# Context statistics through DRAM, and two normal forms of the context made from its transposed copy

## The chip, the cores and the metric

The kernel runs on one core of one Trainium2 chip. The metric is the device time of one execution in microseconds, given as the median of several runs. Batches of the work go through the core one behind the other in an overlapped pipeline, so the steady time of one batch counts 64 times.

## What is computed

There are 64 sequences (`B`) of 128 rows (`S`) and 256 features (`D`), an input `x` and a context of the same shape, and all arithmetic is fp32. Four cross-attention layers stand in a row. Cut to what matters here:

```python
# layer 0: two 16-head attentions (x on x, then x1 on context), three layer norms, fc1/fc2
# layer 1:
h  = rmsnorm(x, ln1_w);  kv = rmsnorm(context, ln1_w)
k, v = kv @ Wk, kv @ Wv                      # 4 key/value heads of 64, rope on q and k
x  = x + attention(h @ Wq, k, v) @ Wo;  x = x + (silu(n @ Wgate) * (n @ Wup)) @ Wdown   # n = rmsnorm(x)
# layer 2:
q  = layer_norm(x);      c  = layer_norm(context, gkv, betakv)
K, V = c @ Wk + bk, c @ Wv + bv
x  = x + attention(q @ Wq + bq, K, V) @ Wo + bo
# layer 3: attention on the plain context with a mask factor and a clip, then a layer norm
```

So the context is wanted in four forms: times a 0/1 row mask (layer 0, second attention), RMS-normed (layer 1), layer-normed (layer 2) and plain (layer 3). The gains and offsets of the norms are folded into weights and biases at the start.

## The kernel before, in words

**Batches.** One batch is one sequence. Its activations stay in SBUF in one of `G` = 4 slots (`g = b % 4`). The attentions are numbered `a` = 0 to 4. Each step of a batch is an event: `queries`, `keys`, `scores`, `soft` (mask, maximum and exponentials, in four units), `turn` (transposes of a unit's probabilities, four units), `values`, `attended` (transposes back and the division), `zT` and `o` (output projection), `tr` (transposes of the inputs of the next attention), and for the dense parts `q2`, `kv2`, `o2`, `x2T`, `h`, `z`, `nT`, `gate`, `up`, `down`. Below, "turn 2.3" is the event `turn` of attention 2, unit 3.

**Order.** The order on each engine is written out by hand. `LIFE` (line 76) gives every event a number for each engine that it uses. `order(engine)` (line 205) adds `PERIOD * b` for batch `b`, sorts all events of all batches, and each engine's program walks through its own sorted list. The numbers only sort; they are no times of the chip. At one time four batches are in work. TensorE's program is `tensor_program`, and the other four queues wait on semaphores for it and for each other.

**PSUM.** Everything but scores goes through `gen_ps`, `N_GEN` = 4 banks in turn, in the order of TensorE's list. A bank's next use waits until its reader has released it (`begin`, `bank_read`); the names in `BANK_LATE` ask for the bank before the other waits of their step.

**The context before.** `ctx_norms` on VectorE makes mean and variance of each context row (lines 1061 to 1066), on GpSimd it makes two factors (`crstd`, line 788) and the RMS-normed context `ctx_rms` (line 809), row by row in the layout rows x features. `tr 2` on TensorE transposes two halves of `zn` (the query side) and two halves of `ctx_rms` (the helper `transposes`, line 459, says line 459 for every transpose), ScalarE copies all four out (`copy_out`, line 699, 512 wide), and `q2` and `kv2` (helper `product`, line 467) multiply them with weights. When `tr 2` has read `ctx_rms`, `ctx_ln` on GpSimd writes the layer-normed context into the same buffer (line 814), and `tr 3` transposes `zn` and that. Attention 4 takes the plain context from `ctxT`, which is loaded already transposed. `x_in`, the loaded `x`, shares the buffer of `ctx_rms`, and `add_residual` (line 796) is its last reader.

**GpSimd's other work.** Each norm takes its reciprocal root from GpSimd (line 788), in the events `stats`, `z`, `mean_square`, `down` and `o 4`; `q2` and `kv2` there finish the rotation, `prob_norm` (line 849) divides the probabilities of attention 2, and `down` and `o 3` prepare the next residuals (lines 856, 860). VectorE's norms in between are `norm` and `norm_x3` (lines 945 and 948), `rms_norm` (line 1096) and `norm_x4` (line 1127).

**Loads.** SyncE waits for a finished output (line 1180), stores it, and then issues six loads for the batch that takes the slot (lines 1155 to 1162).

```python
                elif name == "tr" and a == 2:
                    pe.wait_ge(sem("n3"), b + 1)
                    pe.wait_ge(sem("ctx_rms"), b + 1)
                    transposes("tr2", b, halves(zn[:, g, :]) + halves(ctx_rms[:, g, :]))
```

## Time and profile before

| | |
|---|---|
| median of 3 runs | 4097.45 us (4096.05 to 4101.04) |
| the profiled execution's own time | 4097.15 us |
| its span, first to last instruction | 4095.3 us |
| granted TensorE clock, mean | 0.989 |
| TensorE busy (PE) | 3961.5 us, 97% |
| weight loads (PEld), beside PE | 3439.0 us, 84% |
| VectorE busy | 2890.5 us, 71% |
| ScalarE busy | 2659.4 us, 65% |
| GpSimd busy | 1231.2 us, 30% |
| data moved by DMA | 69.61 MB, mean 17 GB/s |

The busy shares are means over the whole span. PE and PEld are two halves of TensorE: the matmuls proper and the loads of their stationary operand, which run ahead beside them. Matmuls overlap each other, so a group's mean duration is longer than the step from one to the next; the step is read from the start times of a timeline. A fp32 matmul leaves two records, a transpose one.

### The profile page before, as it was taken

To read this page: it belongs to the slowest core of one execution; us is meant where nothing else is said; L and a number is where in the kernel's file an instruction comes from. 1 tells how busy PE (TensorE), PEld (TensorE's weight loads), DVE (VectorE), ACT (ScalarE), POOL (GpSimd) and SP (SyncE) were. 2 spreads that over 40 slices of the span, in tenths; PEclk is the share of its full clock that TensorE was granted. 3 is DMA by queue.
4 is the path that set the end of the run, shared out by engine and by line. 5 is a ranking of instruction groups with operands and counts; after the bars stand their busy time and mean duration, and the time that the engine had idled before them with its cause. 6 is when DMAs were issued, how large, how long until landed. Compare 5 with 4: busy or idle time off the path is not lost.

```text
span 4095.3 us, 115148 instructions
## 1 busy us (share of the span) xinstructions
PE 3961.5 (97%) x44448; PEld 3439.0 (84%) x44448; DVE 2890.5 (71%) x10721; ACT 2659.4 (65%) x8449; POOL 1231.2 (30%) x2247
## 2 busy tenths in 40 slices
...
DMA packets 66495, 69.61 MB, mean 17 GB/s; under 512 B 7456, under 2 KB 64800, under 8 KB 65056
## 3 DMA queue, kind: packets, MB, share of 16 engines
...
q14 instruction: 188, 1.54, 0.1%
...
## 4 chain that ended last, share of the span: by engine, by line
PE 55%; DVE 32%; issue 7%; POOL 3%; ACT 3%; DMA 1%; SPq 0%; DVEq 0%; POOLq 0%; ACTq 0%
PE gen_ps L467 34%; PE gen_ps L459 10%; DVE masked L971 4%; DVE negmax L977 4%; PE scores_ps L549 3%; PE gen_ps L601 3%; DVE st L937 2%; DVE zn L932 2%; DVE masked L964 2%; PE gen_ps L589 2%; PE scores_ps L556 2%; PE scores_ps L563 2%; POOL rstd L788 1%; POOL res L796 1%; DVE rdenm L929 1%
## 5 line engine op out<-in xcount | busy, mean ns | idle before, releaser
L467 PE MATMUL gen_ps<-actT,w_sb 128*128 128x128 f32 x10752 | 1390.1, 279 | 28.9 <-DVE wide L1110 13.5
L467 PEld LDWEIGHTS gen_ps<-actT,w_sb 128*128 128x128 f32 x10752 | 1285.8, 192 | 107.2 <-issue 51.5
L699 ACT ACTIVATE probT<-gen_ps 128x512 f32<-128x512 f32 x1024 | 585.5, 642 | 293.8 <-PE gen_ps L459 293.8
L788 POOL TENSOR_TENSOR rstd<-ve,consts 128x1 f32<-128x1 f32 x448 | 282.6, 631 | 1521.2 <-DVE ve L939 772.1
L733 ACT ACTIVATE prob<-scores_ps,negmax 128x128 f32<-128x128 f32 x2048 | 561.6, 432 | 189.3 <-DVE negmax L977 189.3
L459 PE MATMUL gen_ps<-consts,prob 128*128 128x128 f32 x4096 | 594.4, 278 | 16.1 <-ACT prob L733 6.4
L459 PEld LDWEIGHTS gen_ps<-consts,prob 128*128 128x128 f32 x4096 | 469.8, 142 | 129.2 <-ACT prob L733 58.2
L699 ACT ACTIVATE actT<-gen_ps 128x256 f32<-128x256 f32 (+1 forms) x512 | 235.7, 460 | 383.8 <-PE gen_ps L459 377.3
L467 PE MATMUL gen_ps<-w_sb,actT 128*128 128x256 f32 x1792 | 465.4, 383 | 3.8 <-ACT actT L699 2.8
L849 POOL TENSOR_SCALAR prob<-prob,rden 128x128 f32<-128x128 f32 x1024 | 358.8, 372 | 358.6 <-DVE rden L1050 358.6
L467 PE MATMUL gen_ps<-w_sb,wide 128*128 128x256 f32 x2056 | 465.7, 379 | 0.8 <-DVE wide L1117 0.4
L467 PEld LDWEIGHTS gen_ps<-w_sb,wide 128*128 128x128 f32 x2056 | 385.9, 190 | 51.4 <-issue 1.0
L730 ACT ACTIVATE prob<-masked,negmax 128x128 f32<-128x128 f32 x1024 | 396.0, 394 | 0.0
L977 DVE TENSOR_REDUCE negmax<-scores_ps 128x4 f32<-128x512 f32 x512 | 329.4, 685 | 90.6 <-ACT prob L733 60.0
L467 PEld LDWEIGHTS gen_ps<-w_sb,actT 128*128 128x128 f32 x1792 | 308.4, 192 | 28.9 <-ACT actT L699 4.1
L727 ACT ACTIVATE prob<-masked,negmax 128x128 f32<-128x128 f32 x1024 | 311.9, 394 | 7.3 <-DVE negmax L964 7.3
L589 PE MATMUL gen_ps<-probT,v 128*32 128x128 f32 x8192 | 279.3, 277 | 7.5 <-ACT probT L722 5.1
L699 ACT ACTIVATE oT<-gen_ps 128x512 f32<-128x512 f32 x256 | 154.1, 602 | 189.3 <-PE gen_ps L589 189.3
L1104 DVE TENSOR_TENSOR xs<-gen_ps,xs 128x256 f32<-128x256 f32 x64 | 27.2, 425 | 335.9 <-PE gen_ps L467 335.9
L589 PEld LDWEIGHTS gen_ps<-probT,v 128*32 128x32 f32 x8192 | 209.7, 110 | 45.4 <-issue 20.7
L964 DVE CUSTOM_DVE_ANT_0 masked<-scores_ps,mask 128x128 f32<-128x128 f32 x1024 | 228.9, 286 | 5.4 <-PE scores_ps L549 4.0
L964 DVE CUSTOM_DVE_ANT_0 masked<-scores_ps,consts 128x128 f32<-128x128 f32 x1024 | 228.8, 280 | 2.6 <-PE scores_ps L563 2.6
...
## 6 DMA issues: line engine op xcount, KB each, us to landing
actT<-xT_dram SPq DMA_DIRECT2D x64, 128.0 KB, 2.2
ctx_rms<-x_dram SPq DMA_DIRECT2D x64, 128.0 KB, 2.2
ctx<-ctx_dram SPq DMA_DIRECT2D x64, 128.0 KB, 2.3
ctxT<-ctxT_dram SPq DMA_DIRECT2D x64, 128.0 KB, 2.3
mask<-mask_dram SPq DMA_DIRECT2D x128, 64.0 KB, 2.1
out_dram<-res SPq DMA_DIRECT2D x64, 128.0 KB, 1.7
w_sb<-weights_dram SPq DMA_DIRECT2D x2, 2048.0 KB, 18.6
...
```

The source lines that it names most:

```text
L459: last = nc.tensor.transpose(ps[:, k * P:(k + 1) * P], src, ident)
L467: last = nc.tensor.matmul(ps, lhsT(c), rhs(c), start=(c == 0), stop=(c == chunks - 1))
L589: last = nc.tensor.matmul(ps[32 * k:32 * k + 32, u * S:(u + 1) * S], v16[:, b % G, HU * u + k, :], probT[:, u, k, :], start=True, stop=True)
L699: release(nc.scalar.activation(dst, take(act, name, b)[:, 0:width], ACT.Copy), name, b)
L727: ins = nc.scalar.activation(prob[:, N % 4, k, :], masked[:, N % 3, k, :], ACT.Exp, bias=negmax[:, N % 4, k:k + 1], scale=-1.0)
L730: ins = nc.scalar.activation(prob[:, N % 4, k, :], masked[:, N % 3, k, :], ACT.Exp, scale=-1.0, bias=negmax[:, N % 4, k:k + 1], accum_out= ...
L733: ins = nc.scalar.activation(prob[:, N % 4, k, :], scores_ps[:, u, k * S:(k + 1) * S], ACT.Exp, bias=negmax[:, N % 4, k:k + 1])
L788: nc.gpsimd.tensor_tensor(dst, src, const("expo")[:, 0:width], ALU.pow)\
L849: ins = nc.gpsimd.tensor_scalar(prob[:, N % 4, k, :], prob[:, N % 4, k, :], rden2[:, N % 4, k:k + 1], 0.0, ALU.mult, ALU.add)
L964: ins = nc.vector.tensor_tensor_reduce(out=masked[:, N % 3, k, :], in0=ps[:, k, :], in1=mask1[:, g, :] if a else const("causal"), scale=-1 ...
L971: link(nc.vector.tensor_tensor(masked[:, N % 3, :, :], ps, fT[:, g, :].unsqueeze(1).to_broadcast([P, HU, S]), ALU.mult))
L977: ins = nc.vector.tensor_reduce(negmax[:, N % 4, :], ps, AX.X, ALU.max, negate=True)
```

## The change

The rows of statistics go to all partitions, so that the context can be normed in the transposed layout:

- GpSimd adds a third number to each row's two factors: minus mean times reciprocal deviation (`crstd[..., 2]`, semaphore `cshift`).
- SyncE (`spread_stats`) waits for it, writes the three numbers of all 128 rows into a new DRAM tensor (`stat_d`, turned round: three rows of 128), waits until that has landed, and reads them back to all 128 partitions (`stat_bc`). It does so for batch `b - 1` behind the loads of batch `b`.
- On GpSimd a new event `ctx_rms` makes the RMS-normed transposed context (`ctx_nT`, in the old buffer of `ctx_rms`) as `ctxT` times a broadcast row; `ctx_ln`, once `kv2` has been multiplied, makes the layer-normed one with a multiplication and an addition.
- TensorE's `tr 2` and `tr 3` transpose the two halves of `zn` only; `kv2` and `keys 3` read `ctx_nT`. ScalarE's copies of both are 256 wide and no longer 512.
- `LIFE`, `ONCE` and `PERIOD` have new numbers, `BANK_LATE` is empty, and a scratch area of the DMA set-up is given as 8192 bytes.

```diff
-PERIOD = 71.632128
+PERIOD = 71.742705
...
-    ("ctx_norms", 0, 0, {"DVE": 112.468, "POOL": 79.369}),
+    ("ctx_norms", 0, 0, {"DVE": 90.054, "POOL": 100.780}),
+    ("ctx_rms", 2, 0, {"POOL": 103.794}),
...
-BANK_LATE = {"t32", "t33"}
+BANK_LATE = set()
...
-        crstd = sb("crstd", [P, G, 2])
+        crstd = sb("crstd", [P, G, 3])
+        stat_bc = sb("stat_bc", [P, G, 3, S])
...
+                elif a == 3:
+                    pe.wait_ge(sem("ctx_ln"), b + 1)
                 else:
                     inputs_ready(a, b)
                 ready(f"v{a}")
-                src = ctxT[:, g, :, :] if a == 4 else actT[:, g, 2:4, :]
+                src = ctxT[:, g, :, :] if a == 4 else ctx_nT[:, g, :, :] if a == 3 else actT[:, g, 2:4, :]
...
                     pe.wait_ge(sem("n3"), b + 1)
-                    pe.wait_ge(sem("ctx_rms"), b + 1)
-                    transposes("tr2", b, halves(zn[:, g, :]) + halves(ctx_rms[:, g, :]))
+                    transposes("tr2", b, halves(zn[:, g, :]))
                 elif name == "tr" and a == 3:
                     pe.wait_ge(sem("n4"), b + 1)
-                    pe.wait_ge(sem("ctx_ln"), b + 1)
-                    transposes("tr3", b, halves(zn[:, g, :]) + halves(ctx_ln[:, g, :]))
+                    transposes("tr3", b, halves(zn[:, g, :]))
...
                 elif name == "kv2":
-                    read_out(pe, "tr2", b)
+                    pe.wait_ge(sem("ctx_rms"), b + 1)
...
-                    width = D if a == 4 else 2 * D
+                    width = 2 * D if a == 1 else D
...
                 if name == "ctx_norms":
-                    rsqrt(cve[:, g, :], crstd[:, g, :], "cve", "crstd", b, 2)
+                    rsqrt(cve[:, g, :], crstd[:, g, 0:2], "cve", "crstd", b, 2)
                     pool.wait_ge(sem("crstd"), b + 1)
-                    nc.gpsimd.tensor_scalar(ctx_rms[:, g, :], ctx[:, g, :], crstd[:, g, 1:2], 0.0,
-                                            ALU.mult, ALU.add).then_inc(sem("ctx_rms"), 1)
+                    nc.gpsimd.tensor_scalar(crstd[:, g, 2:3], cmv[:, g, 0:1], crstd[:, g, 0:1], -1.0,
+                                            ALU.mult, ALU.mult).then_inc(sem("cshift"), 1)
+                elif name == "ctx_rms":
+                    pool.wait_ge(sem(f"stat_in{g}"), 16 * (b // G + 1))
+                    pool.wait_ge(sem("res_0"), b + 1)
+                    once(pool, ctxT_sem(b), 16 * (b // G + 1))
+                    nc.gpsimd.tensor_tensor(ctx_nT[:, g, :, :], ctxT[:, g, :, :],
+                                            stat_bc[:, g, 1, :].unsqueeze(1).to_broadcast([P, C, S]), ALU.mult)\
+                        .then_inc(sem("ctx_rms"), 1)
                 elif name == "ctx_ln":
-                    j, use = plan["tr2", b]
+                    j, use = plan["kv2", b]
                     once(pool, bank_full[j], use)
-                    nc.gpsimd.tensor_scalar(ctx_ln[:, g, :], ctx[:, g, :], cmv[:, g, 0:1], crstd[:, g, 0:1],
-                                            ALU.subtract, ALU.mult).then_inc(sem("ctx_ln"), 1)
+                    nc.gpsimd.tensor_tensor(ctx_nT[:, g, :, :], ctxT[:, g, :, :],
+                                            stat_bc[:, g, 0, :].unsqueeze(1).to_broadcast([P, C, S]), ALU.mult)\
+                        .then_inc(sem("ctx_scaled"), 1)
+                    pool.wait_ge(sem("ctx_scaled"), b + 1)
+                    nc.gpsimd.tensor_tensor(ctx_nT[:, g, :, :], ctx_nT[:, g, :, :],
+                                            stat_bc[:, g, 2, :].unsqueeze(1).to_broadcast([P, C, S]), ALU.add)\
+                        .then_inc(sem("ctx_ln"), 1)
...
+                def spread_stats(b):
+                    sp.wait_ge(sem("cshift"), b + 1)
+                    with nc.allow_non_contiguous_dma(reason="three numbers a row"):
+                        sp.dma_start(stat_d[b].rearrange("k s -> s k"), crstd[:, b % G, :])\
+                            .then_inc(sem(f"stat_out{b % G}"), 16)
+                    sp.wait_ge(sem(f"stat_out{b % G}"), 16 * (b // G + 1))
+                    sp.dma_start(stat_bc[:, b % G, :, :].rearrange("p k s -> p (k s)"),
+                                 stat_d[b].rearrange("k s -> (k s)").partition_broadcast(P))\
+                        .then_inc(sem(f"stat_in{b % G}"), 16)
...
+                spread_stats(0)
                 for b in range(2, B + G):
...
+                    if b <= B:
+                        spread_stats(b - 1)
```

**First place: TensorE, turn 2 to out 2.** In these rows `prob` is a unit of four turns, `plainT,q` is `first_row`, `pen,pick` and the row behind it are `scores 1`, `xs` is `tr 4`, and `actT,w_sb x4` is `queries 4`. Before, from the turns 2.0 and 2.1 on:

```order
L459 MATMUL gen_ps<-consts,prob 128x128 x8
L459 MATMUL gen_ps<-consts,xs 128x128 x2
L542 MATMUL scores_ps<-pen,pick 128x128 x16
L563 MATMUL scores_ps<-plainT,wide 128x128 x16
L459 MATMUL gen_ps<-consts,prob 128x128 x4
L467 MATMUL gen_ps<-actT,w_sb 128x128 x4
L459 MATMUL gen_ps<-consts,prob 128x128 x4
L601 MATMUL gen_ps<-probT,v 64x512 x4
```

Now, from turn 2.0 on:

```order
L461 MATMUL gen_ps<-consts,prob 128x128 x4
L469 MATMUL gen_ps<-plainT,q 128x128 x2
L461 MATMUL gen_ps<-consts,prob 128x128 x4
L546 MATMUL scores_ps<-pen,pick 128x128 x16
L567 MATMUL scores_ps<-plainT,wide 128x128 x16
L461 MATMUL gen_ps<-consts,prob 128x128 x4
L461 MATMUL gen_ps<-consts,xs 128x128 x2
L461 MATMUL gen_ps<-consts,prob 128x128 x4
L605 MATMUL gen_ps<-probT,v 64x512 x4
```

`first_row 0` has come in between turn 2.0 and turn 2.1, `tr 4` stands behind `scores 1` and turn 2.2, and `queries 4` has left the stretch; it stands further back, behind turn 1.0.

**Second place: GpSimd, from attended 1 to the residuals.** Before:

```order
L796 TENSOR_TENSOR res<-zn,xs 128x256 [waits bank_read0]
L788 TENSOR_TENSOR rstd<-ve,consts 128x1 [waits ve_1]
L814 TENSOR_SCALAR ctx_rms<-ctx,cmv,crstd 128x256 [waits bank_full1]
L788 TENSOR_TENSOR rstd<-ve,consts 128x1 [waits ve_m]
L788 TENSOR_TENSOR rstd<-ve,consts 128x1 [waits ve_2]
L788 TENSOR_TENSOR rstd<-ve,consts 128x1 [waits ve_4]
L856 TENSOR_TENSOR res<-xs,rows_sb 128x256
L860 TENSOR_TENSOR res<-xs,rows_sb 128x256 [waits bank_read1]
```

Now:

```order
L798 TENSOR_TENSOR res<-zn,xs 128x256 [waits bank_read2]
L817 TENSOR_TENSOR ctx_rms<-ctxT,stat_bc 128x256 [waits ctxT_in1,res_0,stat_in1]
L790 TENSOR_TENSOR rstd<-ve,consts 128x1 [waits ve_1]
L790 TENSOR_TENSOR rstd<-ve,consts 128x1 [waits ve_m]
L823 TENSOR_TENSOR ctx_rms<-ctxT,stat_bc 128x256 [waits bank_full0]
L827 TENSOR_TENSOR ctx_rms<-ctx_rms,stat_bc 128x256 [waits ctx_scaled]
L790 TENSOR_TENSOR rstd<-ve,consts 128x1 [waits ve_2]
L874 TENSOR_TENSOR res<-xs,rows_sb 128x256 [waits bank_read3]
L790 TENSOR_TENSOR rstd<-ve,consts 128x1 [waits ve_4]
L870 TENSOR_TENSOR res<-xs,rows_sb 128x256
```

The new step of line 817 stands ahead of the root of `stats 1` (`ve_1`), the two steps of `ctx_ln` stand between the roots of `z` (`ve_m`) and `mean_square 2` (`ve_2`), and one residual stands ahead of the root of `down` (`ve_4`).

**Third place: SyncE, one batch.** Now:

```order
L1206 DMA out_dram<-res 128x256 [waits out_ready]
L1169 DMA actT<-xT_dram 128x256
L1170 DMA ctx_rms<-x_dram 128x256
L1173 DMA ctx<-ctx_dram 128x256
L1174 DMA ctxT<-ctxT_dram 128x256
L1175 DMA mask<-mask_dram 128x128
L1176 DMA mask<-mask_dram 128x128
L1192 DMA stat_dram<-crstd 128x3x1 [waits cshift]
L1195 DMA stat_bc<-stat_dram 128x384 [waits stat_out0]
```

Before, the first seven stood alone; the last two and their waits are new.

## Rows read from the trace of the kernel before

**Rows 1.** Busy time by stretch: two thousand microseconds of the steady part

```profile
core 0: us, PE busy (x) PEld busy (x) DVE busy (x) ACT busy (x) POOL busy (x), PEclk, DMA share, GB/s
...
2000.00:3000.00 1000.00, 986.32 (x11145) 858.73 (x11143) 725.33 (x2688) 668.19 (x2124) 309.26 (x565) 1.00 0.05 14
```

**Rows 2.** Waits of TensorE by releaser, whole span: us in total, times, longest

```profile
PE gen_ps L459 <- DVE zn L1096: 20.0, 66, 2.9
PE gen_ps L467 <- DVE wide L1110: 13.5, 61, 0.2
PE gen_ps L459 <- DVE xs L1137: 11.8, 63, 0.5
```

**Rows 3.** Waits of the weight loads by releaser, whole span

```profile
PEld gen_ps L459 <- DVEq L903: 19.2, 61, 0.3
```

**Rows 4.** Timeline of PE in one period: start, us, instructions, count, idle before

```profile
2005.52 0.44 PE L459 MATMUL gen_ps<-consts,zn 128*128 128x128 f32 x2 [0.21 <-DVE zn L1096]
2005.79 0.38 PE L459 MATMUL gen_ps<-consts,ctx_rms 128*128 128x128 f32 x2
2006.01 1.03 PE L467 MATMUL gen_ps<-w_sb,actT 128*128 128x256 f32 x4
...
2035.51 1.06 PE L467 MATMUL gen_ps<-actT,w_sb 128*128 128x128 f32 x8
2036.41 0.60 PE L459 MATMUL gen_ps<-consts,prob 128*128 128x128 f32 x4
...
2039.30 1.06 PE L467 MATMUL gen_ps<-ctxT,w_sb 128*128 128x128 f32 x8
...
2041.06 3.62 PE L467 MATMUL gen_ps<-w_sb,wide 128*128 128x256 f32 x16
```

**Rows 5.** Groups of instructions, shapes apart: busy us, mean ns, idle before

```profile
L459 PE MATMUL gen_ps<-consts,ctx_rms 128*128 128x128 f32 x256 | 49.1, 274 | 0.0
L814 POOL TENSOR_SCALAR ctx_rms<-ctx,cmv,crstd 128x256 f32<-128x256 f32 x64 | 77.7, 1214 | 0.3
L809 POOL TENSOR_SCALAR ctx_rms<-ctx,crstd 128x256 f32<-128x256 f32 x64 | 30.7, 479 | 6.3
L796 POOL TENSOR_TENSOR res<-zn,xs 128x256 f32<-128x256 f32 x64 | 46.5, 727 | 328.2 <-DVE zn L932 328.2
L1127 DVE TENSOR_SCALAR zn<-xs,mv,rstd 128x256 f32<-128x256 f32 x64 | 51.7, 808 | 28.4 <-POOL rstd L788 28.4
L1096 DVE TENSOR_SCALAR zn<-xs,rstd 128x256 f32<-128x256 f32 x128 | 44.2, 346 | 2.0 <-POOL rstd L788 2.0
L1132 DVE TENSOR_SCALAR mask<-mask 128x128 f32<-128x128 f32 x64 | 15.8, 246 | 0.0
```

**Rows 6.** Timeline of GpSimd in the same period

```profile
2001.82 0.56 POOL L788 TENSOR_TENSOR rstd<-ve,consts 128x1 f32<-128x1 f32 x1 [7.39 <-DVE ve L939]
2004.08 0.55 POOL L788 TENSOR_TENSOR rstd<-ve,consts 128x1 f32<-128x1 f32 x1 [1.70 <-DVE ve L1091]
...
2033.10 2.80 POOL L849 TENSOR_SCALAR prob<-prob,rden 128x128 f32<-128x128 f32 x8 [1.45 <-DVE rden L1050]
...
2046.47 0.77 POOL L788 TENSOR_TENSOR crstd<-cve,consts 128x2 f32<-128x2 f32 x1
...
2052.89 0.73 POOL L796 TENSOR_TENSOR res<-zn,xs 128x256 f32<-128x256 f32 x1 [5.07 <-DVE zn L932]
2054.56 0.71 POOL L788 TENSOR_TENSOR rstd<-ve,consts 128x1 f32<-128x1 f32 x1 [0.94 <-DVE ve L939]
```

**Rows 7.** DMA issues: count, KB each, median us from issue to landing

```profile
ctx_rms<-x_dram SPq DMA_DIRECT2D x64, 128.0 KB, 2.2
...
out_dram<-res SPq DMA_DIRECT2D x64, 128.0 KB, 1.7
...
rows_sb<-rows_dram SPq DMA_DIRECT2D x1, 1408.0 KB, 9.4
...
cols_sb<-cols_dram SPq DMA_DIRECT2D x1, 13.0 KB, 3.1
```

**Rows 8.** Timeline of VectorE in the same period

```profile
2005.90 0.81 DVE L1127 TENSOR_SCALAR zn<-xs,mv,rstd 128x256 f32<-128x256 f32 x1 [0.44 <-POOL rstd L788]
...
2013.19 0.42 DVE L876 TENSOR_REDUCE absmax<-ctx_rms 128x1 f32<-128x256 f32 x1 [1.13 <-DMA ctx_rms<-x_dram]
```

More of the change, by code:

```diff
@@ new lines @@
+    ("queries", 0, 0, {"PE": 0.000, "DVE": 34.345}),
+    ("keys", 0, 0, {"PE": 16.499, "ACT": 39.357}),
+    ("rows_in", 0, 0, {"DVE": 19.181}),
+    ("first_row", 0, 0, {"PE": 23.029, "DVE": 48.801}),
+    ("scores", 0, 0, {"PE": 49.055}),
+    ("turn", 0, 0, {"PE": 56.029, "ACT": 80.203}),
+    ("turn", 0, 1, {"PE": 57.864, "ACT": 81.988}),
+    ("turn", 0, 2, {"PE": 58.885, "ACT": 82.141}),
+    ("turn", 0, 3, {"PE": 58.899, "ACT": 82.478}),
+    ("values", 0, 0, {"PE": 65.972, "ACT": 89.129}),
@@ new lines @@
+    ("soft", 0, 0, {"ACT": 71.012, "DVE": 68.513}),
+    ("attended", 0, 0, {"PE": 70.183, "DVE": 105.730, "POOL": 69.524}),
+    ("soft", 0, 1, {"ACT": 76.771, "DVE": 75.157}),
+    ("stats", 0, 0, {"DVE": 106.545, "POOL": 75.946}),
+    ("soft", 0, 2, {"ACT": 78.864, "DVE": 76.579}),
+    ("soft", 0, 3, {"ACT": 79.973, "DVE": 77.590}),
+    ("tr", 1, 0, {"PE": 79.259, "ACT": 103.444}),
+    ("norm", 0, 0, {"DVE": 107.100, "POOL": 79.494}),
+    ("queries", 1, 0, {"PE": 80.989, "DVE": 116.258}),
@@ new lines @@
+    ("keys", 1, 0, {"PE": 83.291, "ACT": 109.676}),
+    ("first_row", 1, 0, {"PE": 88.304, "DVE": 116.947}),
+    ("ctx_norms", 0, 0, {"DVE": 90.054, "POOL": 100.780}),
+    ("scores", 1, 0, {"PE": 96.030}),
+    ("attended", 1, 0, {"PE": 113.575, "DVE": 132.961, "POOL": 102.533}),
+    ("ctx_rms", 2, 0, {"POOL": 103.794}),
+    ("turn", 1, 0, {"PE": 105.010, "ACT": 124.984}),
+    ("stats", 1, 0, {"DVE": 134.942, "POOL": 107.017}),
+    ("turn", 1, 1, {"PE": 108.052, "ACT": 132.070}),
+    ("turn", 1, 2, {"PE": 108.456, "ACT": 132.194}),
@@ new lines @@
+    ("ctx_ln", 2, 0, {"POOL": 190.556}),
+    ("down", 3, 0, {"PE": 198.630, "DVE": 225.345, "POOL": 194.705}),
+    ("up", 3, 1, {"PE": 194.916, "DVE": 222.599}),
+    ("rms_norm", 3, 0, {"DVE": 200.053}),
+    ("tr", 3, 0, {"PE": 206.019, "ACT": 229.214}),
+    ("queries", 3, 0, {"PE": 207.744, "DVE": 233.769}),
+    ("keys", 3, 0, {"PE": 208.812, "ACT": 229.956}),
+    ("scores", 3, 0, {"PE": 209.176}),
+    ("turn", 3, 0, {"PE": 216.937, "ACT": 236.727}),
+    ("turn", 3, 1, {"PE": 218.619, "ACT": 238.077}),
```

195 lines of the change are left out of this document (80 added, 115 removed).

## The prediction

> **What bounds the kernel now.** First the busy time by stretch. In the steady part TensorE is busy 986 of 1000 us at a granted clock of 1.00, VectorE 725, ScalarE 668, GpSimd 309 [rows 1]. So TensorE's own work sets the period, and a saving counts there: its instructions, or a wait ahead of one. Then TensorE's waits. Three come once in nearly every batch, about 0.2 us each, all on VectorE: `tr 2` on the normed rows (20.0 us over the run), `up 3.1` on a PSUM bank that `gate 3.1` has not left (13.5), and `tr 4` on the residual (11.8), together 45.3 us [rows 2]. The view of the weight loads shows one more that "busy" hides: inside the four turns of attention 3 the load waits for VectorE's queue to free a bank, 19.2 us in all [rows 3]. Each of these waits is short: VectorE, GpSimd and ScalarE are not full, but their chains end just when TensorE wants them. So the question beside the saved instructions is whether the new order meets those chains better or worse.
>
> **What is removed on TensorE.** 256 transposes of the context go, four a batch. Their group says 49.1 us busy [rows 5], but they overlap their neighbours. The timeline has the step: the pair of `tr 2` starts at 2005.79 and the next matmul at 2006.01, so 0.22 us a pair [rows 4]. Two pairs, 64 batches: **-28.2 us**. `kv2` and `keys 3` keep their shapes and only read another buffer. ScalarE's two copies halve; at 668 of 1000 us busy I cost that at nothing.
>
> **The order on TensorE.** It is much the same list, with moves around the three waits. A whole turn stands in front of `tr 2` that stood behind it, so its normed rows may come 0.4 us later. `scores 0` now stands between `gate 3.1` and `up 3.1`, where it stood before both, and the bank has longer to come free. `tr 4` stands behind `first_row 0`, `scores 1` and turn 2.2. Each move is longer than the wait that it faces, so I take all three out: **-45.3 us**. The bounds are 0 and -45.3. For the turns of attention 3, `mask4` leaves VectorE's stretch just ahead of the steps that free the banks: 246 ns a batch [rows 5], **-15.7 us**, under the 19.2 of the wait; bounds 0 and -19.2.
>
> **New waits on TensorE.** (a) Turn 2.3 needs GpSimd's division. In this period that ended at 2035.90 (2033.10 + 2.80) [rows 6] and turn 2.3 began at 2036.41 [rows 4], 0.51 us of slack. Now `queries 4` (2035.51 to 2036.41, 0.90 us) is gone from in front of it, `first_row 0` (about 0.45, half as many matmuls) has come, and the 0.18 of `tr 4`'s wait goes: 0.63 us earlier. So it waits about 0.12, with a hand-over of 0.1 some 0.25 us: **+16 us**. (b) On GpSimd `ctx_ln` is now two tensor_tensors, 0.73 each by the nearest row [rows 5], in the gap between the root of `z`, done at 2002.38, and that of `mean_square 2`, asked for at 2004.08, a gap of 1.70 [rows 6]. They fit with 0.1 to 0.2 left. The root of `down` comes behind one more residual (0.73), which makes `norm_x4` later. I take 0.1 at `tr 2` and 0.2 at `tr 3`: **+19 us**; bounds 0 and, a piece, 0.46 (below). (c) Moves in ScalarE's and VectorE's lists that I can't follow singly: 0.2 a batch, **+13 us**, one wait of the size of those in rows 2; bounds 0 and three of them.
>
> **GpSimd's load.** It loses 479 + 1214 ns a batch and gains three tensor_tensors of 727 and one single-column step, bounded by nothing and by the two-column root of 0.77 [rows 5, 6]. That is 0.5 to 1.3 us a batch more, at most 2% of the span, on an engine that is busy 31%. By itself it costs nothing.
>
> **The way through DRAM.** The root of the context ends at 2047.24 (2046.47 + 0.77) [rows 6]; with the new single-column step, at most 0.77, SyncE starts at 2048.0 at the latest. No row shows a write in pieces of 4 bytes. The nearest are the store of the output (1.7), the load of the columns, with the shortest rows of all (3.1), and, as the far end, the load of the broadcast rows (9.4) [rows 7]. I take 3.1 for its short rows. The read back is like `x` (2.2). With 0.2 for hand-overs the numbers are there at 2053.5. GpSimd can't use them before `attended 1` is done at 2053.62, and its next root was at 2054.56, behind 0.94 us of idle time [rows 6] in which the 0.73 of the new step fits. Besides, `keys 4` (2039.30 to 2041.06, 1.76 us [rows 4]) now lies between `o 2` and `attended 1` and `first_row 0` no longer does, so the need comes 1.3 us later. Cost nothing; the cover is gone when the write takes over 4.7 us (2048.0 + 4.7 + 2.4 = 2055.1, against 2053.8 + 1.3). The write stands behind the six loads on SyncE, and behind it stands only the next output's wait, a period of 62 us away. On VectorE `ctx_norms` moves to just ahead of the `x` reduction, where the engine idled 1.13 us for the load [rows 8]; it is about as long, so it is covered. The Trainium skill (DMA: Bandwidth & Descriptors, Rules for kernel authors and Specifications) says that a strided last dimension becomes one descriptor for each element, and that pieces under 512 B cost a read-modify-write. By that rule the write, 384 descriptors, belongs to the upper half of the bounds; no run here shows it yet, and what it would do is the third rival.
>
> **The sum.** -28.2 - 45.3 - 15.7 + 16 + 19 + 13 = -41 us on a span of 4095.3, so 4054. The profiled execution's time lies 1.85 above its span and the median of the runs another 0.3 above that: **4056 us**. The forecast's own range is 4025 to 4080, from (a) to (c) at nothing, and from half of the waits still there.
>
> **Rivals.**
>
> 1. *Every wait goes and none comes.* 4097.5 - 89.2 = 4008. For it: the moves all point that way. Against: 0.2 us waits show that the chains are everywhere close, and a faster TensorE meets the next one. Chance 0.07.
>
> 2. *The gain is given back to the chains of VectorE and GpSimd.* `norm_x4` takes 808 ns and `rms_norm` 346 for the same shape on the same data [rows 5]; it starts at 2005.90, in the middle of GpSimd's residual steps [rows 8]. So meeting a GpSimd step costs VectorE up to 0.46 us. The change puts three more two-input steps on GpSimd. If two more meetings and a longer `norm_x4` fall on the chain from `z` over `norm_x3` and `rms_norm` to `tr 2` and `tr 3`, 1.4 us are added, against 0.44 of new cover: 0.95 us a batch, 61 us, in place of the 19 of (b), so 4098. Chance 0.22, of which 0.06 faster, 0.08 the same, 0.08 slower. The Trainium skill (SBUF — State Buffer, Who interferes with whom) says why: a VectorE instruction with two SBUF inputs, or in a two-port mode, and a GpSimd instruction that reads SBUF shut each other out for a whole instruction. By a whole 727 ns a meeting the rival's time would be 4148; the trace, with 0.46, has less than that.
>
> 3. *The statistics come late (slower).* GpSimd waits for the landed numbers in `ctx_rms`, and behind that step in its queue stands the root of `stats 1`, behind it `norm 1` on VectorE, `x2T`, `h` and `z` on TensorE. From a write of 4.7 us on, each microsecond is one of TensorE's. Midway between 3.1 and 9.4 the write takes 6.25 and is 1.5 us late: 64 x 1.5 = 99 us, 4155. For it: the tiny pieces. Against: the output's whole 128 KB land in 1.7 us [rows 7], so a fixed part rules. Chance 0.10.
>
> 4. *The change doesn't do what it says.* The order of instructions excludes it on TensorE: the pairs of rows with the context as source are gone from both steps.
>
> **How the numbers follow.** Forecast 0.61, rivals 0.07, 0.22 and 0.10. A measurement of this kernel can tell a change of about 0.2%, 8 us, from none. Faster by more: 0.07 + 0.57 of the forecast + 0.06 = 0.70. Within 8 us: 0.04 + 0.08 = 0.12. Slower: 0.08 + 0.10 = 0.18. The range of 8 in 10 goes from 4022 to 4110. It leaves out the first rival, most of the third and the ends of the second.
>
> **What would show it.** In the profile after: no group of TensorE with `ctx_rms` as a transposed source; the three rows of waits on VectorE (zn, wide, xs) gone or below 5 us each; a new row of turn waits on GpSimd's `prob` of some 10 to 20 us; the write of the statistics landing in under 4.7 us, and GpSimd's `ctx_rms` step not waiting for the DMA. The prediction is wrong if GpSimd waits on `stat_bc` in every batch, or if the waits in front of `tr 2` and `tr 3` have grown beyond 0.5 us a batch.

## The result, and the profile after

| | before | after |
|---|---|---|
| median | 4097.96 us (4 runs) | 4492.39 us (4 runs, 4491.84 to 4493.97) |
| ratio | | 1.0962, 95% interval 1.0943 to 1.0981 |
| span of the profiled execution | 4095.3 us | 4492.2 us |
| mean granted clock | 0.989 | 0.940 |

The kernel became 394 us slower, 6.2 us for each of 64 batches. The forecast was 41 us faster.

From the page of the kernel after: busy time, packets, and the chain of work that ended last.

```profile
PE 4054.7 (90%) x44192; PEld 3521.1 (78%) x44192; DVE 2899.5 (65%) x10721; ACT 2622.4 (58%) x8449; POOL 1279.7 (28%) x2375
...
DMA packets 101312, 82.29 MB, mean 18 GB/s; under 512 B 34080, under 2 KB 99616, under 8 KB 99872
...
PE 67%; DMA 16%; issue 5%; POOL 4%; DVE 4%; ACT 2%; SPq 0%; DVEq 0%; POOLq 0%; ACTq 0%
```

A sixth of the closing chain is now DMA. The packets under 512 B went from 7456 to 34080. PE shows more busy time than before although 256 transposes are gone; the mean granted clock fell from 0.989 to 0.940. The waits by releaser, whole span (us in total, times, longest) of TensorE, the weight loads, GpSimd and SyncE in turn:

```profile
PE gen_ps L461 <- DVE xs L962: 335.9, 64, 7.8
```

```profile
PEld gen_ps L461 <- DVE xs L962: 348.1, 64, 8.0
```

```profile
POOL ctx_rms L817 <- DMA stat_bc<-stat_dram: 416.3, 63, 9.0
```

```profile
SPq L1195 <- DMA stat_dram<-crstd: 402.7, 49, 10.3
```

The three waits of [rows 2] and the one of [rows 3] have gone. One took their place that is seven times their sum: TensorE waits 5.2 us in every batch for `norm 1` on VectorE. One period shows why. GpSimd (against [rows 6]; line 798 is the residual of `attended 1`, the last line the root of `stats 1`):

```profile
2037.64 0.27 POOL L811 TENSOR_SCALAR crstd<-cmv,crstd 128x1 f32<-128x1 f32 x1
2043.82 0.73 POOL L798 TENSOR_TENSOR res<-zn,xs 128x256 f32<-128x256 f32 x1 [5.92 <-DVE zn L946]
2050.75 0.72 POOL L817 TENSOR_TENSOR ctx_rms<-ctxT,stat_bc 128x256 f32<-128x256 f32 x1 [6.19 <-DMA stat_bc<-stat_dram]
2051.43 0.55 POOL L790 TENSOR_TENSOR rstd<-ve,consts 128x1 f32<-128x1 f32 x1
```

SyncE, which moves the statistics:

```profile
2037.93 0.38 SPq L1192 DMA_DIRECT2D stat_dram<-crstd  x1
2045.96 0.33 SPq L1195 DMA_DIRECT2D stat_bc<-stat_dram  x1
```

VectorE, `norm` (lines 959, 962), and TensorE behind it (against [rows 4]):

```profile
2046.11 0.48 DVE L959 SCALAR_TENSOR_TENSOR zn<-res,mv,rows_sb 128x256 f32<-128x256 f32 x1
2052.08 0.48 DVE L962 SCALAR_TENSOR_TENSOR xs<-zn,rstd,rows_sb 128x256 f32<-128x256 f32 x1 [5.48 <-POOL rstd L790]
```

```profile
2052.62 0.69 PE L461 MATMUL gen_ps<-consts,xs 128*128 128x128 f32 x2 [5.04 <-DVE xs L962]
...
2059.20 1.03 PE L469 MATMUL gen_ps<-w_sb,actT 128*128 128x256 f32 x4
```

Read it from the left. SyncE issues the write at 2037.93 and, since it waits for the landing, the read at 2045.96: the write took 8.0 us (over all batches the read is issued 8.3 us behind the write in the median). GpSimd can go on at 2050.75, 4.8 us later. Its root of `stats 1` needs nothing from the DMA, but stands behind `ctx_rms` in the queue; its input was ready when VectorE went on to line 959 at 2046.11, and it ran at 2051.43. Where [rows 6] has 0.94 us of idle time between the residual and that root, there are now 6.19 ahead of `ctx_rms`. `norm` line 962 runs at once, and TensorE's `x2T` after it. The DMA rows agree (against [rows 7]; us from issue to landing at the end; the write has none):

```profile
stat_bc<-stat_dram SPq DMA_DIRECT2D x64, 192.0 KB, 4.8
...
stat_dram<-crstd SPq DMA_DIRECT2D x64, 1.5 KB
```

GpSimd's groups that answer to L814 and L809 of [rows 5] (mean ns behind the comma; line 823 is like these):

```profile
L827 POOL TENSOR_TENSOR ctx_rms<-ctx_rms,stat_bc 128x256 f32<-128x256 f32 x64 | 50.9, 795 | 5.0
...
L817 POOL TENSOR_TENSOR ctx_rms<-ctxT,stat_bc 128x256 f32<-128x256 f32 x64 | 46.3, 724 | 416.3 <-DMA stat_bc<-stat_dram 416.3
```

The busy time by stretch (against [rows 1]; the granted clock is the third number from the right) shows the second part of the loss:

```profile
1000.00:2000.00 1000.00, 912.71 (x10055) 794.51 (x10054) 657.95 (x2430) 598.86 (x1926) 290.07 (x539) 0.95 0.06 16
...
2052.50:2060.00 7.50, 7.38 (x62) 6.49 (x63) 5.25 (x36) 4.82 (x16) 0.00 (x0) 0.64 0.00 0
```

After the wait TensorE is busy again, but at a granted clock of 0.64 on average, most of that stretch at the lower level, 1.2 GHz; in the 5 us behind it, from 2060.00 on, the clock is at 1.00. In all of the 41 batches between 700 and 3500 us the first 5 us behind the wait have a granted clock of 0.50 to 0.57. From the start of `x2T` to that of the group `w_sb,actT` it takes 2052.62 to 2059.20, 6.58 us; the same instructions at full clock take 4.16 (e11 below, 1078.01 to 1082.17). So the wait costs 5.2 us and the clock behind it 2.4.

### The profile page after: what moved, and what is told of

Its sections match the earlier page's. It is cut to its first block, busy times and chain, and to the rows that moved or that the text cites. A ratio compares the mean times of both kernels' runs of the same rounds, so it can differ in the third digit from the quotient of the medians.

```text
span 4492.2 us, 115018 instructions
## 1 busy us (share of the span) xinstructions
PE 4054.7 (90%) x44192; PEld 3521.1 (78%) x44192; DVE 2899.5 (65%) x10721; ACT 2622.4 (58%) x8449; POOL 1279.7 (28%) x2375
## 2 busy tenths in 40 slices
DMA packets 101312, 82.29 MB, mean 18 GB/s; under 512 B 34080, under 2 KB 99616, under 8 KB 99872
## 4 chain that ended last, share of the span: by engine, by line
PE 67%; DMA 16%; issue 5%; POOL 4%; DVE 4%; ACT 2%; SPq 0%; DVEq 0%; POOLq 0%; ACTq 0%
PE gen_ps L469 40%; PE gen_ps L461 14%; DMA stat_dram<-crstd 9%; DMA stat_bc<-stat_dram 6%; PE gen_ps L593 5%; PE scores_ps L567 3%; PE scores_ps L553 3%; PE gen_ps L605 3%; POOL rstd L790 2%; DVE wide L906 1%; POOL ctx_rms L817 1%; POOL crstd L790 1%; ACT oT L701 1%; ACT prob L735 1%; DVE xs L962 1%
## 5 line engine op out<-in xcount | busy, mean ns | idle before, releaser
L469 PE MATMUL gen_ps<-actT,w_sb 128*128 128x128 f32 x9728 | 1296.2, 289 | 12.1 <-DMA w_sb<-weights_dram 8.0
L469 PEld LDWEIGHTS gen_ps<-actT,w_sb 128*128 128x128 f32 x9728 | 1230.7, 204 | 67.4 <-issue 46.4
L701 ACT ACTIVATE actT<-gen_ps 128x256 f32<-128x256 f32 (+1 forms) x512 | 212.0, 414 | 609.8 <-PE gen_ps L461 609.8
L461 PE MATMUL gen_ps<-consts,xs 128*128 128x128 f32 x384 | 97.3, 343 | 345.7 <-DVE xs L962 335.9
L962 DVE SCALAR_TENSOR_TENSOR xs<-zn,rstd,rows_sb 128x256 f32<-128x256 f32 x192 | 117.5, 612 | 437.2 <-POOL rstd L790 437.2
L593 PE MATMUL gen_ps<-probT,v 128*32 128x128 f32 x8192 | 332.3, 312 | 7.9 <-ACT probT L724 5.1
L461 PEld LDWEIGHTS gen_ps<-consts,xs 128*128 128x128 f32 x384 | 47.6, 162 | 371.6 <-DVE xs L962 348.1
L469 PE MATMUL gen_ps<-w_sb,actT 128*128 128x256 f32 x1280 | 334.1, 384 | 3.9 <-ACT actT L701 2.9
L593 PEld LDWEIGHTS gen_ps<-probT,v 128*32 128x32 f32 x8192 | 245.5, 124 | 71.9 <-ACT probT L701 24.6
L713 ACT ACTIVATE plainT<-gen_ps,kbias 128x128 f32<-128x128 f32 x256 | 80.2, 364 | 314.9 <-PE gen_ps L469 314.9
## 6 DMA issues: line engine op xcount, KB each, us to landing
w_sb<-weights_dram SPq DMA_DIRECT2D x2, 2048.0 KB, 19.0
```

The costliest lines, as they stand in the source:

```text
L461: last = nc.tensor.transpose(ps[:, k * P:(k + 1) * P], src, ident)
L469: last = nc.tensor.matmul(ps, lhsT(c), rhs(c), start=(c == 0), stop=(c == chunks - 1))
L593: last = nc.tensor.matmul(ps[32 * k:32 * k + 32, u * S:(u + 1) * S], v16[:, b % G, HU * u + k, :], probT[:, u, k, :], start=True, stop=True)
L701: release(nc.scalar.activation(dst, take(act, name, b)[:, 0:width], ACT.Copy), name, b)
L962: nc.vector.scalar_tensor_tensor(dst, zn[:, g, :], rstd[:, g, 0:1], row(bias), ALU.mult, ALU.add).then_inc(sem(signal), 1)
```

## The experiments

Four theories. **A**: the statistics come late and the GpSimd queue passes that on (the mechanism of the third rival). **B**: the other new work on GpSimd, and its meetings with VectorE, costs the time; a meeting is a GpSimd step that runs at the same time as a VectorE instruction. **C**: the slow transfers themselves disturb the other work. **D**: the new order costs it. Later: why the write takes 8 us, and where the transposes' gain is. "Before" was 4098 to 4099 us beside all of them.

| run | median us | ratio to before |
|---|---|---|
| e1 `ctx_rms` behind the root | 4011.24 | 0.9788 (0.9772 to 0.9805) |
| e2 `ctx_norms` early | 4024.44 | 0.9815 (0.98 to 0.983) |
| e3 no way through DRAM (2 runs) | 4000.24 | 0.976 (0.9741 to 0.978) |
| e4 pieces of 12 bytes (2 runs) | 4005.04 | 0.9772 (0.9752 to 0.9791) |
| e5 pieces of 4 bytes in row order | 4486.92 | one run |
| e6 read of distinct rows | 4002.85 | one run |
| e7 e4 with transposes | 4019.41 | 0.981 (0.9795 to 0.9824) |
| e8 before, new table | 4006.34 | 0.9776 (0.976 to 0.9792) |
| e9 e4, `ctx_ln` moved | 3982.56 | 0.9722 (0.9708 to 0.9737) |
| e10 e8, `ctx_ln` moved | 4000.52 | 0.9764 (0.975 to 0.9779) |
| e11 e4, write issued twice | 4147.18 | one run |
| e12 e4's form, old table | 4097.74 | 0.9994 (0.9984 to 1.0003) |

### e1: `ctx_rms` behind the root of `stats 1`

```diff
-    ("ctx_rms", 2, 0, {"POOL": 103.794}),
+    ("ctx_rms", 2, 0, {"POOL": 107.500}),
```

> One number of the change's table: GpSimd's step ctx_rms sorts behind the root of stats 1 (107.5 in place of 103.794). The trip through DRAM is as slow as before (write 8.0 us, read 4.8 us). Theory A (the harm is what stands behind the waiting step): GpSimd still waits for the numbers until about 2050.7 in the period shown, but the next root behind it, that of z, is wanted only some 11 us later, so TensorE's wait of 5.0 us ahead of x2T goes, and with it the half clock behind it: 4000 to 4060 us. Theory B (three more two-input steps on GpSimd hold VectorE up): the time stays above 4098, since the steps are all there. Theory C (the slow DMA itself disturbs others): stays near 4490.

One number, 481 us. GpSimd in one period (the roots of `stats 1` and of `z`, with `ctx_rms` between them):

```profile
2014.78 0.55 POOL L790 TENSOR_TENSOR rstd<-ve,consts 128x1 f32<-128x1 f32 x1 [1.10 <-DVE ve L953]
2020.03 0.73 POOL L817 TENSOR_TENSOR ctx_rms<-ctxT,stat_bc 128x256 f32<-128x256 f32 x1 [4.70 <-DMA stat_bc<-stat_dram]
2023.76 0.72 POOL L790 TENSOR_TENSOR rstd<-ve,consts 128x1 f32<-128x1 f32 x1 [3.00 <-DVE ve L953]
```

GpSimd still waits 4.7 us for the slow transfer, but with nothing behind it that is wanted, and the wait costs nothing: TensorE is busy 994 of 1000 us at a clock of 1.00. A is shown. B, C and D fall: the change's other work on GpSimd, its slow transfers (the read is issued 8.2 us behind the write in the median and lands 4.8 us later) and its order but for this one step are all still there.

### e2 and e3: the statistics early, and not at all

e2 makes the statistics a phase earlier; e3 takes the transfers out.

```diff
-    ("ctx_norms", 0, 0, {"DVE": 90.054, "POOL": 100.780}),
+    ("ctx_norms", 0, 0, {"DVE": 90.054, "POOL": 52.900}),
```

```diff
+            nc.gpsimd.memset(stat_bc[:, :, :, :], 1.0).then_inc(sem("su_stat"), 1)
...
-                    pool.wait_ge(sem(f"stat_in{g}"), 16 * (b // G + 1))
...
-                    if b <= B:
-                        spread_stats(b - 1)
```

> The other end: GpSimd makes the three numbers of the context right behind VectorE's ctx_norms (52.9 in place of 100.78), some 34 us earlier, so the trip through DRAM has 47 us and not 6. Theory A: GpSimd's wait on stat_bc goes entirely, 4000 to 4060 us, like e1. Theory B: above 4098. If e2 is clearly faster than e1, a part of the cost of the wait remains in e1.

> Leaves out the trip through DRAM: stat_bc is set to ones once at the start, SyncE sends nothing for it, GpSimd waits for nothing there; the normed contexts are then the plain context. All other steps and the order are the change's. Theory A: the same as e2 within 0.3%, 4000 to 4060 us. Theory B: above 4098. What e2 has over e3 is the price of the DMAs themselves.

Both recover the time. In e2 nothing waits for `stat_bc` any more, but TensorE has small waits on VectorE (9.2 and 8.7 us in all) where e3 has 2.8; in the two profiled executions, 17 us apart, that is most of the distance. Taken out altogether (e3), the trip is worth 5 us against e4 and 11 against e1 by the medians; in both cases the intervals overlap.

### e4, e5 and e6: what makes the transfer slow

e4 keeps the three numbers of a row side by side in DRAM, so that the write has 128 pieces of 12 bytes and not 384 of 4; GpSimd then reads the spread numbers with a step of three. e5 has e4's addresses in DRAM, but its source is spread out, so that it has 384 pieces again. e6 is e4 with the read replaced by one of the same size from 128 different rows of the weights; its context norms use those numbers in place of the statistics. The first edit is against the changed kernel, the other two are against e4.

```diff
-        stat_bc = sb("stat_bc", [P, G, 3, S])
+        stat_bc = sb("stat_bc", [P, G, S, 3])
...
-                        sp.dma_start(stat_d[b].rearrange("k s -> s k"), crstd[:, b % G, :])\
+                        sp.dma_start(stat_d[b], crstd[:, b % G, :])\
```

```diff
-                        sp.dma_start(stat_d[b], crstd[:, b % G, :])\
+                        sp.dma_start(stat_d[b], crstd[:, b % G, :, 0])\
```

```diff
-                                 stat_d[b].rearrange("s k -> (s k)").partition_broadcast(P))\
+                                 w_d[:, 384 * (b % 8):384 * (b % 8) + 384])\
```

> The change's order, but the DRAM tensor holds the three numbers of a row side by side: the write is 128 pieces of 12 bytes and not 384 of 4, the read is the same 1536 bytes for each partition, and GpSimd reads the broadcast row with a step of three numbers. If the write's 8.0 us go with its pieces, it takes (8.0 - 1.7) / 3 + 1.7 = 3.8 us, the numbers come 4.2 us earlier, and TensorE's wait of 5.0 us falls to about 0.8: 4120 to 4200 us if the clock holds. If the write is slow for another reason, 4490 as before. If the stepped read slows GpSimd's three steps (0.72 us each now), this shows in their mean.

> As e4 (numbers of a row side by side in DRAM), but they lie 8 bytes apart in SBUF, so the write is again cut into 384 pieces of 4 bytes, now to neighbouring addresses. If the number of pieces makes the write slow, it takes about 8 us again, GpSimd waits for stat_bc in every batch and the time is near 4490. If it is the spread over three DRAM rows that makes it slow, the write lands in about 2.7 us as in e4 and the time is near 4005.

> As e4, but the read takes 128 different rows of 1536 bytes out of the weights in place of one row for all partitions; the normed contexts are then wrong numbers, everything else is there. The read of one row landed in 4.0 us (4.8 in the change), where x lands in 2.2 with 1024 bytes a partition. If the common address makes it slow, it lands in 2.3 to 2.6 us; if the size does, in 4.0 as before. The time stays at about 4005 either way, since GpSimd does not wait for it in e4.

The DMA issues of e4:

```profile
stat_bc<-stat_dram SPq DMA_DIRECT2D x64, 192.0 KB, 4.0
...
stat_dram<-crstd SPq DMA_DIRECT2D x64, 1.5 KB, 2.1
```

The same 1.5 KB land in 2.1 us in the median (3.8 were expected), and TensorE's wait on `xs` falls from 335.9 us to 4.0. With the read's 0.8 us less, the statistics come some 7 us earlier, more than the 5.9 by which they were late, so the time is 4005 and not the 4120 to 4200 expected. The step of three has a small price that the means show: line 823 takes 0.79 us, where its counterpart in e3 takes 0.72 at the same place. e5 is back at 4487 us, and its read is again issued 7.9 us behind the write in the median, against 2.2 in e4: it is how the write is cut, 384 pieces of 4 bytes or 128 of 12, and not where the pieces lie in DRAM. Number and size of the pieces change together, so which of the two counts isn't separated. The Trainium skill (DMA: Bandwidth & Descriptors, Rules for kernel authors) has the rule that a strided last dimension gives a descriptor for each element; the counts agree, 34080 small packets in the changed kernel against 17696 in e4, 16384 or 64 x 256 fewer. The read takes 3.5 us from distinct rows (e6) against 4.0 from one common row: by one run the common address costs 0.5 us at most, for the same read took 3.8 in e12 and 3.7 in e11; the rest is in the transfer's 192 KB and its form. The 4.8 us of the changed kernel are not its DRAM layout either: e5, with e4's layout, has 4.8 too. The read is slower behind a write in 384 pieces; why, no run shows.

### e7 and e8: what the transposes and the table are worth

e7 is e4 with four idle transposes a batch put back (`zn` twice). e8 is the kernel before, with its transposes and no way through DRAM, under the new table (the numbers of `LIFE` and `ONCE` besides the two shown).

```diff
-                    transposes("tr2", b, halves(zn[:, g, :]))
+                    transposes("tr2", b, halves(zn[:, g, :]) + halves(zn[:, g, :]))
...
-                    transposes("tr3", b, halves(zn[:, g, :]))
+                    transposes("tr3", b, halves(zn[:, g, :]) + halves(zn[:, g, :]))
```

```diff
-PERIOD = 71.632128
+PERIOD = 71.742705
...
-BANK_LATE = {"t32", "t33"}
+BANK_LATE = set()
```

> e4 with four transposes a batch put back: tr 2 and tr 3 transpose the halves of zn a second time into the free half of the bank, which nobody reads. This prices the removed TensorE work alone, under the new order. By the step of 0.22 us a pair it is 28 us slower than e4's 4005: 4033. If the transposes had been hidden by waits, 4005; if the waits grow with them, over 4040.

> The kernel before with the new numbers of the order alone (no DRAM trip, all four transposes in tr 2 and tr 3, the context normed in rows by GpSimd). If the order is what removes the three waits on VectorE and part of the bank wait of the turns, it gains the 45 + 16 us that the prediction gave them: about 4037. If the order only fits the new steps, 4098 or more. Together with e7 it says whether the two parts of the gain add up: 28 + 61 = 89 against the 94 of e4.

The table alone gives 91 us, all that e4 has, where 61 were expected. The transposes are worth 14 us in e7, half of the 28 expected, and nothing between e8 and e4. e4 shows what stands in their place, three small waits. VectorE and GpSimd of e4 at that point:

```profile
2014.90 0.93 DVE L962 SCALAR_TENSOR_TENSOR xs<-zn,rstd,rows_sb 128x256 f32<-128x256 f32 x1 [0.51 <-POOL rstd L790]
```

```profile
2014.77 0.78 POOL L823 TENSOR_TENSOR ctx_rms<-ctxT,stat_bc 128x256 f32<-128x256 f32 x1
2015.63 0.87 POOL L827 TENSOR_TENSOR ctx_rms<-ctx_rms,stat_bc 128x256 f32<-128x256 f32 x1
```

`norm_x3` (line 962) takes 0.93 us beside the new step of line 823; the same line takes 0.48 with GpSimd idle (changed kernel, 2052.08). In VectorE's new order `attended 4` stands behind `norm_x3`, and TensorE's `zT 4` needs it. And TensorE, from turn 0.0 over `zT 4` and `tr 2` to `tr 3`:

```profile
2015.86 0.60 PE L461 MATMUL gen_ps<-consts,prob 128*128 128x128 f32 x4
2016.52 0.44 PE L461 MATMUL gen_ps<-consts,zn 128*128 128x128 f32 x2
2016.79 1.47 PE L461 MATMUL gen_ps<-consts,prob 128*128 128x128 f32 x12
...
2018.37 1.03 PE L469 MATMUL gen_ps<-w_sb,actT 128*128 128x256 f32 x4
2019.34 0.44 PE L461 MATMUL gen_ps<-consts,zn 128*128 128x128 f32 x2
```

The first step, 2015.86 to 2016.52, is 0.66 us, where the four transposes take 0.44 in e9 (below); the one ahead of `tr 3`, 2018.37 to 2019.34, is 0.97 against 0.87 in e9. The pair of `zT 4` at 2016.52 takes 0.27 where an unhindered one takes 0.22 [rows 4], and so does that of `tr 2` (2018.10 to 2018.37). Together that is 0.42, nearly the 0.44 removed.

### e9 and e10: `ctx_ln` away from `norm_x3`

```diff
-    ("ctx_ln", 2, 0, {"POOL": 190.556}),
+    ("ctx_ln", 2, 0, {"POOL": 153.500}),
```

> The kernel of e4_rows_of_12_bytes with ctx_ln moved in GpSimd's order (from 190.556 to 153.500), into the idle stretch behind norm 0 and away from VectorE's norm_x3. In e4 norm_x3 (line 962) takes 0.93 us beside the two-input step of line 823, against 0.72 in e8 and 0.49 when nothing stands beside it, and three small waits of TensorE follow (0.22 + 0.10 + 0.07 us a batch). If those are the place where the transposes' gain went, norm_x3 comes back to 0.5 to 0.7 us, the waits go, and the time is 3980, 20 to 25 us below e4. If the cause is another (the order of the two shorter copies on ScalarE, or the weight loads), the time stays at 4005 within 4 us. If the move meets another chain (prob_norm), the time is above 4010.

> The control: the kernel of e8_table_alone (context normed in rows, transposed on TensorE, no way through DRAM) with the same move of ctx_ln. There TensorE waits for neither of the normed rows, so if the gain of e9 is that of the waits, nothing changes here: 4006 within 4 us. If the move helps in itself, this falls by as much as e9 does.

TensorE of e9, the same stretch:

```profile
2006.18 0.60 PE L461 MATMUL gen_ps<-consts,prob 128*128 128x128 f32 x4
2006.62 0.38 PE L461 MATMUL gen_ps<-consts,zn 128*128 128x128 f32 x2
2006.84 1.47 PE L461 MATMUL gen_ps<-consts,prob 128*128 128x128 f32 x12
...
2008.37 1.03 PE L469 MATMUL gen_ps<-w_sb,actT 128*128 128x256 f32 x4
2009.24 0.44 PE L461 MATMUL gen_ps<-consts,zn 128*128 128x128 f32 x2
```

Its group of line 962 (`xs`, three calls a batch, one of them `norm_x3`):

```profile
L962 DVE SCALAR_TENSOR_TENSOR xs<-zn,rstd,rows_sb 128x256 f32<-128x256 f32 x192 | 93.1, 485 | 68.7 <-POOL rstd L790 66.5
```

In e4 the mean of this group was 633 ns. The steps are back at 0.44, 0.22 and 0.87 us, and the time is 22 us below e4, as expected. In the rows form (e10) the same move took `norm_x3` from 0.72 to 0.48 us and gave 6 us by the medians, where at most 4 were expected, with an interval that overlaps e8's; so the move itself is at most about a quarter of e9's gain. Between e10 and e9 lie 18 us: the transposes' worth, of the 28.2 forecast, once nothing takes it back. e9 is the fastest kernel of the study, 2.8% under the kernel before.

### e11: a dose of lateness

Against e4, the write is issued twice, the second behind the landing of the first.

```diff
-                    sp.wait_ge(sem(f"stat_out{b % G}"), 16 * (b // G + 1))
+                    sp.wait_ge(sem(f"stat_out{b % G}"), 32 * (b // G) + 16)
+                    with nc.allow_non_contiguous_dma(reason="three numbers a row"):
+                        sp.dma_start(stat_d[b], crstd[:, b % G, :])\
+                            .then_inc(sem(f"stat_out{b % G}"), 16)
+                    sp.wait_ge(sem(f"stat_out{b % G}"), 32 * (b // G + 1))
```

> A dose: the kernel of e4_rows_of_12_bytes with the write to DRAM issued twice, the second after the first has landed, so that the statistics come about 2.9 us later, against a slack of 0.5. TensorE then waits some 2.4 us a batch. If a microsecond of lateness costs a microsecond, as the prediction's third rival has it: 4005 + 64 x 2.4 = 4159. If a wait of that length also halves the granted clock for a while behind it, as the 5.2 us wait does in the changed kernel (2.3 us lost a batch): up to 4306. The granted clock of the steady part tells which: 1.00 or 0.95.

TensorE's wait of the whole span, two of its periods, and the busy time of the five us behind each:

```profile
PE gen_ps L461 <- DVE xs L962: 110.3, 64, 3.7
```

```profile
1078.01 0.44 PE L461 MATMUL gen_ps<-consts,xs 128*128 128x128 f32 x2 [1.64 <-DVE xs L962]
...
1082.17 1.03 PE L469 MATMUL gen_ps<-w_sb,actT 128*128 128x256 f32 x4
...
1140.56 0.44 PE L461 MATMUL gen_ps<-consts,xs 128*128 128x128 f32 x2 [1.95 <-DVE xs L962]
...
1146.31 1.03 PE L469 MATMUL gen_ps<-w_sb,actT 128*128 128x256 f32 x4
```

```profile
1078.01:1083.01 5.00, 5.00 (x62) 4.51 (x63) 5.00 (x35) 4.45 (x14) 0.00 (x0) 1.00 0.00 0
1140.56:1145.56 5.00, 5.00 (x52) 4.45 (x53) 4.59 (x34) 3.27 (x10) 0.00 (x0) 0.66 0.01 3
```

The wait is 1.7 us a batch, less than the 2.4 expected, so the dose was over-sized by 0.7. The span is 144 us longer than e4's: 106 from the wait, which leaves 38. Behind the wait of 1.64 us the clock stayed at 1.00 and the stretch to `w_sb,actT` took 4.16 us; behind that of 1.95 it was 0.66 and the stretch took 5.75. Of 44 batches in the middle 16 had such a stretch; 16/44 of 64 batches at 5.75 - 4.16 = 1.59 us each is 37, the 38 that are left. None of the 16 waits was under 1.7 us, but behind two others, of 2.09 and 2.56 us, the clock stayed at 1.00: the length of the wait alone doesn't decide it. So a microsecond of lateness costs a microsecond, as the third rival had it, and a clock term comes on top that it had not.

### e12: the new form under the old order

The edit is against e4, with the old numbers of `LIFE` and `ONCE`.

```diff
-PERIOD = 71.742705
+PERIOD = 71.632128
...
-BANK_LATE = set()
+BANK_LATE = {"t32", "t33"}
...
+    ("ctx_rms", 2, 0, {"POOL": 84.500}),
```

> The new form (12-byte rows through DRAM, norms from the transposed context, no transposes) under the order of before, with ctx_rms put in at 84.500 on GpSimd and BANK_LATE as before. If the 256 transposes count where TensorE is fullest: 4098 - 28 = 4070. If the chains of VectorE and GpSimd give it back, as the second rival of the prediction has it: 4098 or above. The three waits of rows 2 should still be there in either case.

The three waits of TensorE, and VectorE's `norm 1` with GpSimd's `ctx_rms` beside it:

```profile
PE gen_ps L461 <- DVE zn L1110: 20.2, 66, 2.6
PE gen_ps L469 <- DVE wide L1124: 13.2, 60, 0.2
PE gen_ps L461 <- DVE xs L1151: 11.8, 63, 0.5
```

```profile
2056.20 0.94 DVE L962 SCALAR_TENSOR_TENSOR xs<-zn,rstd,rows_sb 128x256 f32<-128x256 f32 x1 [0.51 <-POOL rstd L790]
```

```profile
2056.07 0.79 POOL L817 TENSOR_TENSOR ctx_rms<-ctxT,stat_bc 128x256 f32<-128x256 f32 x1
```

The same instruction of VectorE in the kernel before, beside the one-input step of line 814:

```profile
2055.38 0.72 DVE L948 SCALAR_TENSOR_TENSOR xs<-zn,rstd,rows_sb 128x256 f32<-128x256 f32 x1 [0.51 <-POOL rstd L788]
```

TensorE around it, from the group ahead of `x2T` over `x2T` and `values 4` to the next group, in e12:

```profile
2055.21 2.05 PE L469 MATMUL gen_ps<-actT,w_sb 128*128 128x128 f32 x16
...
2058.73 1.13 PE L469 MATMUL gen_ps<-actT,w_sb 128*128 128x128 f32 x8
```

and in the kernel before:

```profile
2054.39 2.05 PE L467 MATMUL gen_ps<-actT,w_sb 128*128 128x128 f32 x16
...
2057.69 1.13 PE L467 MATMUL gen_ps<-actT,w_sb 128*128 128x128 f32 x8
```

4097.74 us: the 28 are given back whole. The period shown has two places for it. `norm 1` is 0.22 us longer (0.94 against 0.72), and TensorE's stretch around `x2T`, which needs it, is 0.22 us longer: 3.52 against 3.30. And `tr 3` wants `norm_x4`, which takes 0.81 us as before, now 0.22 us earlier, since the pair of `tr 2` is gone from in front of it: the step ahead of it is 0.98 us (2006.88 to 2007.86) against 0.87 before, and its pair 0.27 against 0.21. Together 0.39 of the 0.44 removed. The three waits stand as in [rows 2]. `norm_x3` itself takes 0.48 us in both kernels. So the loss is of the second rival's kind, the VectorE chain beside two-input steps of GpSimd, but with one meeting and at another place. No run moved `ctx_rms` away from `norm 1` under the old order, so this account is read from the steps and not tested.

## Why the prediction was wrong

- **The failing step: "The way through DRAM".** It took the write for 3.1 us, and it is 8.0; the read for 2.2, and it is 4.8. The working around these two numbers holds: with them the statistics are there at 2048.0 + 8.0 + 4.8 + 0.2 = 2061.0 against a need at 2055.1, 5.9 us late, and TensorE's wait is 5.2, 336 us over the run, where the prediction had nothing. Its own sign of being wrong, GpSimd waiting on `stat_bc` in every batch, is there (416.3 us, 63 times). The choice was made between a load of 3.1 and one of 9.4 by the length of its rows, but the row compared is 128 rows of 104 bytes (13 KB) and the write has 384 pieces. The read was set equal to `x` although it moves 192 KB and not 128. And "against" the third rival stood the store of 128 KB in 1.7 us, as if a fixed part ruled; it is 128 rows of 1 KB.
- **The third rival** had the right mechanism, place and queue, and the wrong price and chance: 1.5 us late and 0.10. It put the write midway at 6.25 us and left the read alone.
- **No term for the clock.** A stall was costed at its own length. It is 5.2 us and 2.4 more behind it, together about the 7.5 a batch (481 / 64) that lie between the changed kernel and e1.
- **The three waits, -45.3, and the bank of turn 3, -15.7: right in kind, too small.** All four went. The new table alone is worth 91 us (e8), where these two terms make 61; that the rest of the 91 comes from the same four waits is argued and not tested, since the table moves more than them. The view of the weight loads of the kernel before has more: its waits on `zn` are

```profile
PEld gen_ps L459 <- DVE zn L1096: 61.5, 128, 3.1
```

  where PE has 20.0, on `xs` 27.2 and on `wide` 25.1; with the 19.2 of [rows 3] that is 133, and PE's rows with it 64.5. The measured 91 lies between, so here PE's rows alone gave too little and the loads' rows too much.
- **(a) Turn 2.3, +16: wrong.** No such wait came (1.1 us in all on GpSimd's `prob` in e8 and in the changed kernel).
- **(b) +19 for `tr 2` and `tr 3`: right in kind, half in size.** In e4 the pair of `tr 2` is 0.05 us longer and the step ahead of `tr 3` 0.10, 10 us in all. The load of `tr 3` waits 24.2 us in the changed kernel, but still 17.9 in e9, whose gain of 22 us over e4 is mostly the next term's.
- **(c) +13 for what could not be followed singly: it is there.** In e4 `zT 4` comes 0.22 us a batch late, 14 us, because `attended 4` now stands behind the longer `norm_x3` on VectorE.
- **The transposes, -28.2:** 14 in e7, 18 from e10 to e9, 0 from e8 to e4 and from before to e12. The step is what the trace said; whether it counts is up to the VectorE chain.
- **The second rival** was real, and hidden in the result. Under the new table it took back most of the 28: e4 is level with e8, and e9, with `ctx_ln` away from `norm_x3`, is 18 us below e10. Its price holds on line 962: 0.48 us alone, 0.87 to 0.88 beside a GpSimd step in the changed kernel and 0.93 in e4, 0.39 to 0.45 a meeting where it had up to 0.46. The rows that it took the price from don't show it by themselves: `norm_x4` takes 0.81 us in every run and always runs beside a residual. Under the old order (e12) all of the 28 went, but by one meeting with `norm 1` and by `norm_x4` as it was. The Trainium skill (SBUF — State Buffer, Who interferes with whom) has the two-input instruction of VectorE and GpSimd's shut each other out; the step of line 823 had 0.65 us to go when line 962 began (2014.77 + 0.78 - 2014.90), so by that line 962 would take some 0.65 + 0.48 = 1.13 us here, an estimate. It took 0.93: the trace shows the meeting, and at a lower price.
- **ScalarE's and GpSimd's loads at nothing: right.** GpSimd gained 49 us, 0.76 a batch, inside the bounds.

What stays open: why the read takes 4.8 us behind 384 pieces and 4.0 behind 128; which part of its 3.5 us in e6 is its 192 KB and which its 1536-byte rows; whether e12's 28 us come back once `ctx_rms` is moved; and the 10 us between the 18 that the transposes gave and the 28.2 of their steps. The last 0.06 us wait at `tr 3` of e9 is a part of that.
